# Storing and loading turned queries and keys by quads of heads in a fused attention and expert kernel

## The reference, cut to what matters

```python
B, S, D, H = (4, 512, 256, 16)      # 16 heads of 16 values, 1024 keys per batch
...
query = split_heads(q @ w_q.T)
key_ = split_heads(k @ w_k.T)
value = split_heads(v @ w_v.T)
query = _rope(query)
key_ = _rope(key_)
scores = jnp.einsum('bhqd,bhkd->bhqk', query, key_) / np.sqrt(DK)
scores = jnp.where(mask[:, None, None, :] == 0, -10000.0, scores)
attn = jax.nn.softmax(scores, axis=-1)
x = jnp.einsum('bhqk,bhkd->bhqd', attn, value)
```

## Time and profile before

| | us |
|---|---|
| median of 3 runs | 861.96 |
| lowest and highest of them | 859.24 and 866.88 |
| profiled execution, its own time | 859.62 |
| span of the profiled execution | 857.8 |

### The profile page before, as it was taken

The page is one execution under the profiler, slowest core; times in us unless marked ns, Lnnn a source line. Parts: engine busy times, 40 slices in busy tenths (PEclk is TensorE's granted clock), DMA queues, the critical chain, the costliest instruction groups (busy, mean ns, idle before and its releaser), DMA issues. The chain is left out here.

```text
span 857.8 us, 12963 instructions
## 1 busy us (share of the span) xinstructions
PE 690.1 (80%) x4120; PEld 408.6 (48%) x4120; DVE 569.3 (66%) x972; ACT 491.9 (57%) x954; POOL 364.4 (42%) x272
## 2 busy tenths in 40 slices
PE   3347889998899998998889988457776329999996
PEld 3233334433444334442333322347676318888885
DVE  5947876777877777778778752348777624555553
ACT  2011567777677775676656678265643225666663
POOL 4973606284052770143998920000142522444434
PEclk9675899999999999999999999568967658999999
DMA  9674454967448560238787820298312835533321
GB/s 262 208 207 143 161 189 139 267 212 224 123 150 250 196 197 17 76 110 225 244 278 269 275 98 1 67 351 337 56 57 62 276 90 130 111 35 38 36 31 19
DMA packets 60261, 133.31 MB, mean 155 GB/s; under 512 B 8996, under 2 KB 25940, under 8 KB 58740
## 3 DMA queue, kind: packets, MB, share of 16 engines
q1 hardware_dynamic: 33396, 73.51, 26.4%
q0 software_dynamic: 17360, 37.92, 17.3%
q10 hardware_dynamic: 9440, 21.06, 8.4%
HBM read 82.11 MB, written 70.70 MB: 178 GB/s over the span
## 5 line engine op out<-in xcount | busy, mean ns | idle before, releaser
L713 DVE TENSOR_REDUCE mx<-wide 128x2 f32<-128x1024 f32 x256 | 306.9, 1223 | 96.7 <-PE wide L836 95.8
L581 ACT ACTIVATE probs<-narrow 128x512 f32<-128x512 f32 x512 | 277.3, 598 | 104.1 <-PE narrow L863 101.8
L863 PE MATMUL narrow<-qst,kst 51*128 51x512 f32 x512 | 171.0, 475 | 19.5 <-ACT probs L581 13.9
L836 PE MATMUL wide<-kst,qst 49*128 49x512 f32 x512 | 156.4, 468 | 22.8 <-DMA kst<-k_pieces 9.6
L863 PEld LDWEIGHTS narrow<-qst,kst 51*128 51x128 f32 x512 | 72.0, 188 | 175.0 <-ACT probs L581 121.6
L878 PE MATMUL values<-probs,vaug 128*17 128x512 f32 x1024 | 137.7, 610 | 0.7 <-ACT probs L581 0.7
L1557 POOL DMA_INDIRECT out<-res,token x39 | 61.6, 1580 | 98.9 <-DMA out<-res,token 59.9
L836 PEld LDWEIGHTS wide<-kst,qst 49*128 49x128 f32 x512 | 65.1, 196 | 44.2 <-DVE mx L713 28.2
L431 POOL TENSOR_TENSOR turn_b<-turn_a,tab 128x1024 f32<-128x1024 f32 x10 | 24.2, 2417 | 116.9 <-ACT turn_a L575 116.3
L1130 POOL DMA_DIRECT2D out<-h x4 | 5.3, 1337 | 131.4 <-DVE h L1313 131.4
L1582 ACT ACTIVATE h_hi<-narrow 128x512 fp32r<-128x512 f32 x39 | 23.3, 598 | 46.3 <-PE narrow L1659 46.3
(11 more groups left out here) (253 smaller groups left out, 1313.0 us busy)
## 6 DMA issues: line engine op xcount, KB each, us to landing
list_rows<-in_w ACTq DMA_DIRECT2D x56, 342.0 KB, 5.1
kst<-k_pieces SPq DMA_DIRECT2D x14, 784.0 KB
k_pieces<-turn_a SPq DMA_DIRECT2D x16, 512.0 KB, 4.7
w_hi<-w_hi SPq DMA_DIRECT2D x16, 512.0 KB, 11.6
w_lo<-w_lo SPq DMA_DIRECT2D x16, 512.0 KB, 12.3
qst<-q_pieces SPq DMA_DIRECT2D x14, 384.0 KB
turn_a<-in_w POOLq DMA_DIRECT2D x10, 512.0 KB, 5.6
w_hi<-turn_b POOLq DMA_DIRECT2D x10, 512.0 KB, 3.0
```

The costliest lines, as they stand in the source:

```text
L581: nc.scalar.activation(probs[:, n % NP, :], narrow[ring_no["score", n] % 3][:, :], ACT.Exp, scale=DK ** -0.5).then_inc(exp_done, 1)
L713: last = nc.vector.tensor_reduce(mx[quad % 2][:, qt, :, hp, kh], slot[:, :, :], axis=AX.X, op=ALU.max)
L836: last = nc.tensor.matmul(slot[:, i, :], qst[u % 3][r:r + R_MAX, h, P * qt:P * qt + P], kst[u % 3][r:r + R_MAX, h, 512 * kh:512 * kh + 512 ...
L863: nc.tensor.matmul(narrow[ring_no["score", n] % 3][:, :], kst[u % 3][r:r + R_ALL, h, P * kt:P * kt + P], qst[u % 3][r:r + R_ALL, h, :], st ...
```

## The change

The weights' columns, the table of cosines and sines and the two DRAM tensors are put in an order in which each quad of heads owns 32 neighbouring partitions of `turn_a` and `turn_b`. `store_turned` then writes one quad at a time: 12 DMAs of 32 partitions (128 KB each) for a block, in place of 3 of 128 partitions (512 KB each). Each set has two semaphores, `turned_first` for quad 0 and `turned_out` for quads 1 to 3, and whoever waited for a stored block waits for both, except the loads of quad 0. `load_queries` and `load_keys` read a quad at a time, so that a unit takes four DMAs for each in place of two. The mask row takes 16 DMAs in place of 4. The amounts of data are the same.

In the list of SyncE's calls, the three blocks of batch 0 are stored in two parts: quad 0 of (0, 2), (0, 1) and (0, 0), with the loads of quad 0 between them, and then, behind the load of context (1, 1), quads 1 to 3 of (0, 1), (0, 0) and (0, 2). All other blocks are stored whole.

```diff
-            for n, src in enumerate((turn_a, turn_a, turn_b) if part == 2 else (turn_a, turn_b, turn_a)):
-                if part == 2:
-                    dst = q_dram[b, n].rearrange("e p t -> p e t")
-                else:
-                    dst = k_dram[b, DK * n:DK * n + DK, :, 512 * part:512 * part + 512].rearrange("(e d) h t -> (d h) e t", e=2)
-                sp.dma_start(dst, src[i][:, :, :]).then_inc(turned_out[i], 16)
...
+            for quad in range(0 if first else 1, 4 if rest else 1):
+                for n, src in enumerate((turn_a, turn_a, turn_b) if part == 2 else (turn_a, turn_b, turn_a)):
+                    if part == 2:
+                        dst = q_dram[b, quad, DK * n:DK * n + DK]
+                    else:
+                        dst = k_dram[b, quad, DK * n:DK * n + DK, :, 512 * part:512 * part + 512]
+                    sp.dma_start(dst.rearrange("(e d) x t -> (d x) e t", e=2), src[i][32 * quad:32 * quad + 32, :, :]).then_inc((turned_first if quad == 0 else turned_out)[i], 16)
...
         load_context(1, 0)
-        store_turned(0, 2)
-        store_turned(0, 1)
+        store_turned(0, 2, rest=False)
+        store_turned(0, 1, rest=False)
         load_keep(1, 0)
-        load_queries(0, slice(0, 2))
-        load_keys(0, slice(0, 2), (1,))
-        load_queries(0, slice(2, PAIRS))
-        store_turned(0, 0)
-        load_keys(0, slice(0, 2), (0,))
-        load_keys(0, slice(2, PAIRS))
+        load_queries(0, [0])
+        load_keys(0, [0], (1,))
+        store_turned(0, 0, rest=False)
+        load_keys(0, [0], (0,))
         load_context(1, 1)
+        store_turned(0, 1, first=False)
+        store_turned(0, 0, first=False)
+        store_turned(0, 2, first=False)
+        load_queries(0, [1])
+        load_keys(0, [1])
         load_queries(1)
         load_keys(1)
...
                 if set_before(block_of):
-                    act.wait_ge(*sets_stored(set_before(block_of)))
+                    for stored_part in sets_stored(set_before(block_of)):
+                        act.wait_ge(*stored_part)
```

More of the change, by code:

```diff
@@ L175, in cross_attention @@
     maxrow_in = [sem(f"maxrow_in{i}") for i in range(2)]
-    turned_out = [sem(f"turned_out{i}") for i in range(3)]
+    turned_first, turned_out = [[sem(f"turned_{n}{i}") for i in range(3)] for n in ("first", "out")]
     values_prepared, filled = sem("values_prepared"), sem("filled")
@@ L303, in load_keep, with store_turned, stored, landed @@
             sp.dma_start(keep[n % 2][:, :].bitcast(I32), io["mask"].rearrange("(b k) p -> b (k p)", b=B)[b:b + 1, 512 * g:512 * g + 512].to_broadcast([P, 512])).then_inc(keep_in[n % 2], 16)
-        def store_turned(b, part):
+        def store_turned(b, part, first=True, rest=True):
             sp.wait_ge(*by_turner(("rope", b, part)))
             i = set_of(b, part)
-            for n, src in enumerate((turn_a, turn_a, turn_b) if part == 2 else (turn_a, turn_b, turn_a)):
-                if part == 2:
-                    dst = q_dram[b, n].rearrange("e p t -> p e t")
-                else:
-                    dst = k_dram[b, DK * n:DK * n + DK, :, 512 * part:512 * part + 512].rearrange("(e d) h t -> (d h) e t", e=2)
-                sp.dma_start(dst, src[i][:, :, :]).then_inc(turned_out[i], 16)
[L316 to L320, removed]
+            for quad in range(0 if first else 1, 4 if rest else 1):
[5 more added lines that the diff above has]
+                    sp.dma_start(dst.rearrange("(e d) x t -> (d x) e t", e=2), src[i][32 * quad:32 * quad + 32, :, :]).then_inc((turned_first if quad == 0 else turned_out)[i], 16)
+        def stored(b, part, quads=range(4)):
+            for first, done in zip((0, 1), sets_stored(("rope", b, part))):
+                if (0 in quads) if first == 0 else (quads != [0]):
+                    sp.wait_ge(*done)
+        def landed(u, h):
+            return quad_in if u == 0 and h == 0 else stack_in[u % 3]
         def freed(u):
@@ L324, in freed, with load_queries, load_keys @@
                 sp.wait_ge(score_ready, 64 * (u - 2))
-        def load_queries(u, heads=slice(0, PAIRS)):
+        def load_queries(u, heads=(0, 1)):
             b, c = divmod(u, 2)
             freed(u)
[L330 to L335, removed]
+            stored(b, 2, [2 * c + h for h in heads])
+            for h in heads:
+                for i in range(2):
+                    sp.dma_start(qst[u % 3][HALF * i:HALF * i + R_MASK, 2 * h:2 * h + 2, :].bitcast(F32), q_dram[b, 2 * c + h, :, 2 * i:2 * i + 2, :]).then_inc(landed(u, h), 16)
+        def load_keys(u, heads=(0, 1), parts=(0, 1)):
             b, c = divmod(u, 2)
@@ L339, in load_keys @@
             for part in parts:
-                stored(b, part)
+                stored(b, part, [2 * c + h for h in heads])
             if c == 0:
-                sp.wait_ge(shut_out[b], 16)
+                sp.wait_ge(shut_out[b], 64)
             tokens = slice(512 * parts[0], 512 * parts[-1] + 512)
-            k = k_dram[b].rearrange("r (c i h) t -> c i r h t", c=2, i=2)[c]
-            for i in range(2):
-                sp.dma_start(kst[u % 3][HALF * i:HALF * i + R_MAX, heads, tokens].bitcast(F32), k[i][:, heads, tokens]).then_inc(landed(u, heads), 16)
+            for h in heads:
+                for i in range(2):
+                    sp.dma_start(kst[u % 3][HALF * i:HALF * i + R_MAX, 2 * h:2 * h + 2, tokens].bitcast(F32), k_dram[b, 2 * c + h, :, 2 * i:2 * i + 2, tokens]).then_inc(landed(u, h), 16)
         def load_table(half):
@@ L488, in _ @@
         for i in range(2):
-            pool.wait_ge(*sets_stored([j for j in in_sets if set_of(*j[1:]) == i][-1]))
+            for stored_part in sets_stored([j for j in in_sets if set_of(*j[1:]) == i][-1]):
+                pool.wait_ge(*stored_part)
         pieces = [(io["wqkv"], KC, QKV, split_dram["wqkv"]), (io["wproj"], KC, D, split_dram["wproj"])]
@@ L593, in _ @@
         act.wait_ge(ones_in, 12 * 16)
-        act.wait_ge(*sets_stored(("rope", 0, 2)))
+        for stored_part in sets_stored(("rope", 0, 2)):
+            act.wait_ge(*stored_part)
         for w in ("v", "o"):
```

18 lines of the change are left out of this document (10 added, 8 removed).

## The result

| | before | after |
|---|---|---|
| median of 4 runs, us | 861.67 | 880.29 |
| lowest and highest, us | 859.24 and 866.88 | 876.04 and 885.25 |
| profiled execution, its own time, us | 859.62 | 880.88 |
| its span, us | 857.8 | 879.1 |

The ratio of after to before is 1.0211, with a 95% interval from 1.0165 to 1.0256. The kernel became slower by about 2%. The forecast was 868.0 with a range of 858 to 876, "within 1%" as the likeliest case: the sign was right, the size was not, and the median lies above the range.

The account below looks back on a forecast made before the run. It took the start as the bound: the first quad's keys and three other chains ahead of the first score. First score +6.2, rest 0, taken as +6: 865.6 on the profiled execution, 868.0 on the median, range 858 to 876.

Parts of the forecast that it names:

- Mask row: SyncE at the start: 12 more DMAs at 0.66 us, ending near 28.7, hidden by VectorE until 32.45; cost 0.
- First maximum: VectorE, first quad: keys issued at 49.0, so it runs at about 54 in place of 61.23, gaining 7 us.
- The held copy: ScalarE's copy of k (1, 0, 0), ready at 50.25, waits until all of block (0, 1) is stored, at 60.5.
- T: Time when the nine late stores of block (0, 1) have landed and ScalarE can copy: 60.5, between 57 and 62.
- k (1, 1, 0): TensorE, after GpSimd's block (1, 0) and context split: can start at 80.6 against 78.84, losing the 7 us and 1.8 more.
- Row of maxima: SyncE's queue: issued at 84.8, lands behind the remaining loads at about 92; first score 92.0 against 85.84, +6.2 us.
- rival A: At the first score, the row doesn't wait for the queue, or the bulk moves at full rate: 861, chance 0.22.
- The mask for (1, 1): Last of the loads in SyncE's queue; GpSimd starts at about 91.5 against 84.56, +7, in step with the rest.
- The step that failed: Later batches: nine more issues per block, 5.5 us of SyncE, covered by waiting, and four loads for two: both 0.
- Rival B: After the start, second row of maxima and block (1, 1) come too late, lead used up: +11, 873, chance 0.25.
- the first score's delay: Start of the attention's steady part: first score at 92.0 in place of 85.84, +6.2 us, taken as +6.
- Rival C: At the start the gain of 7 us is kept, ScalarE not held, nine stores landed by 53: 855, chance 0.03.

Follow-up runs that it names:

- e10_halves: The changed kernel with a block's 12 stores going through the quads in the order 0, 2, 1, 3 within each of three pieces: 875.05 us, ratio 1.0125.
- e1_rows_ahead: The changed kernel with first row of maxima and mask (1, 1) ahead of unit 1's loads, every fourth quad's row ahead of next unit's keys: 860.96 us, ratio 0.9973.

## Why the prediction was too small, by its own steps

- **Mask row**, cost 0: right. The 16 issues took 5.60 us, not 10.6, since the shorter DMAs are issued in 0.35 us each; hidden either way.
- **First maximum** at about 54: 54.05.
- **The held copy**, T = 60.5 (57 to 62): 58.90, and 8.37 us of waiting for the stores, the wait that was named.
- **k (1, 1, 0)** at 80.6: about 78.9, when GpSimd's split ends (76.48 + 2.34); 1.6 early with T. The rate of 200 GB/s behind T was read where the context's load of 128 partitions was under way too; the ports measured alone gave 203. The 7 us gained by the maxima are lost here, as said.
- **Row of maxima** issued at 84.8, landed at 92.0: issued at 82.95, score at 91.90. The row waits for the bulk ahead of it, which refutes rival A (0.22). The hit within 0.1 us is luck in part: the loads behind the 27 stores were issued at 68.59, not 70, and from there to the first score it took 23.3 us, not 22.
- **The mask for (1, 1)**: "+7, in step with the rest". It landed 18.8 us after its issue at 73.85, GpSimd started at 92.78, 8.2 us later. Quad 1's row was ready at 115.23 (ScalarE's copy 114.64 + 0.59), and SyncE, busy with the stores until then, issued it at 116.84: the slack of 3.8 us is used up and 1.6 more, but no score waited for it. The cost is 0, as taken.
- **The step that failed** is this: "In later batches each block costs nine more issues, 5.5 us of SyncE, which mostly waits for ScalarE; the wait for the next row of maxima covers them, 0. The four loads for two of a unit: 0." I priced SyncE's time and not the queue behind it. The issues are covered, but the stores' drain is longer, the loads start 3 us later, four more issues lengthen the queries' loads from 1.72 to 3.90 us, and what was left of the lead, 13.9 us between the keys' issue and the row's, fell to 8.0. (The lead alone isn't the whole: `e10_halves` had 9.8 us of it, and quad 11 still waited 6.36. With the keys behind the row the wait was gone.) In the first batch I had let the row land behind the bulk, with the earlier trace rows as the reason; I didn't ask the same question three times more, at quads 3, 7 and 11. Where the sum had 0, the runs show this: quad 11's wait of 6.60 us in the changed kernel and 7.58 in its second profile, where 1.85 was before, and 0.9% of the time, about 8 us, won back by moving the later rows (1.0063 to 0.9973). In the ledger of the first profile it is more, +6.8 to quad 4 and +9.8 to quad 11, but the step at quad 3 depends on the execution.
- **Rival B** ("the delay grows", 0.25) had the sign and a range that came near (873), but not the place: it saw the second row, quad 1, at the edge. That quad's scores didn't wait; those of quads 3 and 11 did, behind the queries' round trip, which B doesn't name.
- The sum also had no term for what follows a wait. The waits grew by 14.8 us, the ledger by 24.2 at quad 15. And the first score's delay, forecast rightly at 6 us, is worth 9 to 13 us when it is taken away with what hangs on it (the runs with one move). The granted clock at 0.50 behind the hole goes with that difference, but its share wasn't isolated: the clock falls about there without a wait for a row too, to 0.81 from 425 to 430 us before and to 0.56 in `e1_rows_ahead`. This stays open.
- **Rival C** (0.03), the gain kept, didn't occur, but the version that beats both shows that part of it was to be had: with the nine stores in SyncE's gap and the row ahead, 852.76.

What is shown: the place of the row behind the bulk makes the loss (1.021 to 0.997 by two moves, with the small DMAs and the held copy still there), quad 11's wait is independent of the first (1.006 with the first move alone), and small DMAs in the order of before cost 1.1%. What is argued: that the mask, which moves with the first row, has no part in it; and what makes quad 11 wait most. Its row follows the one before it sooner than those of quads 3 and 7 (23.6 us against 28.3 and 28.4), and GpSimd's seven DMAs run only there; no run changed the one or the other. What is open: why the time grows by more than the waits.

## What to carry to other kernels

An edit that cuts DMAs into more and smaller ones is priced by the time until the queue has drained behind them, at each place where a small urgent transfer stands in the same queue, and not by the issuing engine's time. Put the urgent one ahead of the bulk in program order, above all where the bulk isn't needed soon: here this was worth 2.4%, and with it the idea of storing the first quad early paid, once its late stores had moved too. And when a gate of the start is modelled with care, go with the same model through every later repetition of the pattern before writing a 0.

## What the runs showed of the hardware that I hadn't expected

- Stores from 32 and from 64 neighbouring partitions both move about 205 GB/s with all 16 DMA engines busy, and 128 move 422. Two groups of 32 from different halves, one behind the other in one queue, start at 195 and reach 285 and 352 in the two stretches shown: neighbours in the queue do overlap.
- A small DMA behind loads of 49 partitions, which keep only 0.45 of the engines busy while they move 188 GB/s, still waits for them: from issue to use the rows of quads 0, 3 and 11 took 9.0, 10.4 and 14.2 us, and the mask, which stood behind them too, landed after 18.8.
- Loads of 48 partitions keep all engines busy (share 1.03) and move 184 GB/s, loads of 49 keep 0.45 of them busy and move 178: a fuller share isn't a faster load here.
- A DMA of the mask row is issued by SyncE in 0.35 us (5.60 for 16), against 0.66 for the four larger ones of before.
